# One recurrent layer: the final addition goes into an accumulating transfer, the root becomes logarithm and exponential, small products take rows of their own, and a turn stands amid the gate

## What is computed

```python
xa = _ln(x, ln1_w, ln1_b)
sx = shifted(xa) - xa
t = tanh((xa + sx * maa_x) @ maa_w1).reshape(B, L, 5, -1)          # 5 groups of 32
mw, mk, mv, mr, mg = (t[:, :, j] @ maa_w2[j] for j in range(5))     # the mixtures
xw, xk, xv, xr, xg = (xa + sx * (maa_j + mj) ...)
w = exp(-exp(time_decay + tanh(xw @ decay_w1) @ decay_w2))          # 64 wide inside
r, k, v, g = xr @ Wr.T, xk @ Wk.T, xv @ Wv.T, silu(xg @ Wg.T)
# per head of 16: s_new = k v + w * s ; out = r . (faaaa * k v + s)
y = (y - gm) * rsqrt(gv + EPS) * gn_w + gn_b
x = x + y * g @ Wo.T
xc = _ln(x, ln2_w, ln2_b); sxc = shifted(xc) - xc
rr = sigmoid((xc + sxc * fmaa_r) @ fWr.T)
kk = square(relu((xc + sxc * fmaa_k) @ fWk.T))
x = x + rr * (kk @ fWv.T)
```

## Time and profile before

| what | us |
|---|---|
| median of 3 runs | 3539.14 |
| lowest, highest | 3535.2, 3544.54 |
| the profiled execution, its own time | 3535.91 |
| its span | 3534.1 |
| granted TensorE clock, mean | 0.968 |
| busy in the span: PE, DVE, ACT, POOL | 3319.9, 2390.6, 1787.9, 196.2 |
| this layer | about 1400 to 2320 of the span |

### The profile page before, as it was taken

The page is one execution under the profiler, slowest core; times in us unless marked ns, Lnnn a source line. Parts: engine busy times, 40 slices in busy tenths (PEclk is TensorE's granted clock), DMA queues, the critical chain, the costliest instruction groups (busy, mean ns, idle before and its releaser), DMA issues. The chain is left out here.

```text
span 3534.1 us, 55156 instructions
## 1 busy us (share of the span) xinstructions
PE 3319.9 (94%) x21472; PEld 2547.0 (72%) x21472; DVE 2390.6 (68%) x3781; ACT 1787.9 (51%) x4255; POOL 196.2 (6%) x311
## 2 busy tenths in 40 slices
PE   7999999999999997889999998679999999699998
PEld 6777888887777785656666665357788788488885
DVE  6666666666665665499999999637777887642213
ACT  4555444444454443456565554427777777532222
POOL 0000000000000000000000000001111111000000
PEclk9999999999999999899999999879999999899999
DMA  5332212231122211544444444120001110210004
GB/s 215 124 105 107 108 72 76 97 115 72 72 96 90 78 73 57 156 114 103 111 108 102 114 103 108 41 108 3 35 31 70 44 48 31 88 53 24 24 12 162
DMA packets 93456, 296.08 MB, mean 84 GB/s; under 512 B 20016, under 2 KB 28208, under 8 KB 68752
## 3 DMA queue, kind: packets, MB, share of 16 engines
q1 hardware_dynamic: 64896, 186.47, 18.0%
q0 software_dynamic: 10368, 75.50, 5.6%
q10 hardware_dynamic: 17936, 30.59, 2.5%
HBM read 233.82 MB, written 58.72 MB: 83 GB/s over the span
## 5 line engine op out<-in xcount | busy, mean ns | idle before, releaser
L537 ACT ACTIVATE l_prob<-l_bank,l_nmax 128x512 f32<-128x512 f32 x512 | 345.3, 687 | 276.8 <-DVE l_nmax L679 276.8
L679 DVE TENSOR_REDUCE l_nmax<-l_bank 128x1 f32<-128x512 f32 x512 | 317.5, 682 | 71.4 <-PE l_bank L409 71.2
L375 PE MATMUL l_bank<-l_x_hi,l_w_hi 128*128 128x256 f32 x1024 | 298.0, 291 | 11.7 <-DVE l_x_lo L779 11.7
L702 DVE COPY l_probT<-l_bank 128x512 f32<-128x512 f32 x256 | 173.7, 689 | 175.3 <-PE l_bank L423 173.2
L375 PE MATMUL l_bank<-l_x_hi,l_w_lo 128*128 128x256 f32 x1024 | 290.9, 284 | 0.0
L375 PE MATMUL l_bank<-l_x_lo,l_w_hi 128*128 128x256 f32 x1024 | 290.7, 284 | 0.0
L1752 DVE TENSOR_TENSOR_SCAN l_kv<-l_wx,l_kv 128x2056 f32<-128x2056 f32 x64 | 283.8, 4434 | 1.6 <-DVE first_nrs L1765 1.2
L2320 ACT ACTIVATE l2a_sc<-l2a_sc,l2a_nmax 128x256 f32<-128x256 f32 x512 | 254.8, 508 | 41.1 <-DVE l2a_nmax L2436 41.1
L423 PE MATMUL l_bank<-l_ident,l_prob 128*128 128x128 f32 x2048 | 247.9, 275 | 10.7 <-DVE l_k_lo L695 6.3
L423 PEld LDWEIGHTS l_bank<-l_ident,l_prob 128*128 128x128 f32 x2048 | 225.8, 141 | 24.4 <-DVE l_k_lo L695 16.3
L445 PE MATMUL l_bank<-l_probT,l_v 128*64 128x512 f32 x1024 | 233.8, 598 | 0.0
(11 more groups left out here) (353 smaller groups left out, 8207.5 us busy)
## 6 DMA issues: line engine op xcount, KB each, us to landing
l_vb<-vd SPq DMA_DIRECT2D x64, 1024.0 KB
l_w_hi<-kept_w_hi POOLq DMA_DIRECT2D x24, 1024.0 KB, 8.2
l_w_lo<-kept_w_lo POOLq DMA_DIRECT2D x24, 1024.0 KB, 10.2
l_wv_hi<-kept_wv_hi POOLq DMA_DIRECT2D x12, 1024.0 KB, 5.1
l_wv_lo<-kept_wv_lo POOLq DMA_DIRECT2D x12, 1024.0 KB, 7.1
kept_w_hi<-l_w_hi SPq DMA_DIRECT2D x8, 1024.0 KB, 8.8
kept_w_lo<-l_w_lo SPq DMA_DIRECT2D x8, 1024.0 KB, 11.2
l2a_x<-x SPq DMA_DIRECT2D x16, 512.0 KB, 3.8
```

Source lines behind the costliest of these rows:

```text
L375: mm = pe.matmul(s.ap[:, c * ROWS:(c + 1) * ROWS], a[:, kt, c, g, :], b[:, kt, c * ROWS:(c + 1) * ROWS], start=m == 0, stop=m == 3 * KT - 1)
L537: act.activation(prob[h][:, it, :], s.ap[:, :], ACT.Exp, bias=nmax[:, n % 2, it, h:h + 1], accum_out=rsum[:, n % 2, it, h:h + 1]).then_inc ...
L679: dve.tensor_reduce(nmax[:, n % 2, it, h:h + 1], s.ap[:, :], AX.X, ALU.max, negate=True).then_inc(max_ready, 1)
L702: dve.tensor_copy(probT[0][:, j, :], s.ap[:, :]).then_inc(s.drained, 1)
```

## The change

Five edits, all in `l1_layer`:

- **Transfer.** The sum `xres` (x plus the Wo product) is stored to `x2` by ACT as soon as it is made (`store_res`, ahead of `stats_c`), the product rr * (kk @ fWv) is written by `out_part` to `rv`, a view of the tile `sxc`, and POOL issues a transfer that adds `rv` to `x2` in memory (`add_out`, at the end of its round, after waits for `res_stored` and `rv_ready`). DVE's addition L1872 and ACT's `store` go. `shift_c`, which writes `sxc`, now waits for that transfer of the round before.
- **Logarithm.** `roots` takes Ln and then Exp with scale -0.5 on ACT; DVE's reciprocal `inverse` goes.
- **Row halves.** `decay_w1` is held twice side by side, so that `decay_in` gives its 64 results in partitions 0 to 63 and again in 64 to 127, and `decay_out` takes its first half of channels from rows 0 to 63 and the other from rows 64 to 127, in turn.
- **Turning amid the gate.** The turn of xc stands between the two halves of `project g` on PE, and so in `ring`.
- **Mixtures of v and g together.** v lies in rows 64 to 95; g moves from rows 64 to 95 of `w2b` and `tT` to rows 0 to 31, and the products of the two alternate, where mixture v stood.

```diff
-        ring += [f"mv{p}_0", f"mv{p}_1"] if p is not None else []
+        ring += [f"m{n}{p}_{half}" for half in H2 for n in "vg"] if p is not None else []
         ring += [f"bn{r}_0", f"bn{r}_1"] if r is not None else []
-        ring += [f"mg{p}_0", f"mg{p}_1"] if p is not None else []
         ring += [f"nc{q}_0", f"nc{q}_1"] if q is not None else []
         ring += [f"o{c}_0", f"o{c}_1"] if c is not None else []
         ring += [f"v{p}_0", f"v{p}_1"] if p is not None else []
         ring += [f"nv{q}"] if q is not None else []
         ring += [f"mw{p}_0", f"mw{p}_1"] if p is not None else []
+        ring += [f"g{p}_0"] if p is not None else []
         ring += [f"xc{c}_0", f"xc{c}_1"] if c is not None else []
-        ring += [f"g{p}_0", f"g{p}_1", f"mk{p}_0", f"mk{p}_1", f"d{p}"] if p is not None else []
+        ring += [f"g{p}_1", f"mk{p}_0", f"mk{p}_1", f"d{p}"] if p is not None else []
...
-        dw1 = ph.sb("dw1", [P, CT, 64])
+        dw1, dw2 = ph.sb("dw1", [P, CT, P]), ph.sb("dw2", [P, ROWS])
...
+        rv = sxc[:, :, :].rearrange("p c t -> p (c t)").rearrange("p (r n) -> p r n", r=RT)
...
-                        sp.wait_ge(out_stored, 16 * c)
+                        sp.wait_ge(res_stored, 16 * c)
...
+                def add_out(c):
+                    pool.wait_ge(res_stored, 16 * (c + 1))
+                    pool.wait_ge(rv_ready, 2 * c + 2)
+                    pool.dma_start(x2[c].rearrange("(r p) n -> p r n", p=P), rv, accum_op=ALU.add).then_inc(out_added, 16)
...
+                    if b >= 1:
+                        add_out(b - 1)
+                pool.wait_ge(out_added, 16 * B)
...
-                def mixture(p, n):
-                    f = MIX.index(n)
-                    lhs, own, at = (w2a, slice(32 * f, 32 * f + 32), 0) if f < 4 else (w2b, slice(64, 96), 1)
+                def mixture(p, *names):
+
                     pe.wait_ge(t_ready, p + 1)
                     for half in H2:
-                        s = S[f"m{n}{p}_{half}"]
-                        free(pe, s)
+                        for n in names:
+                            free(pe, S[f"m{n}{p}_{half}"])
                         for ct in (2 * half, 2 * half + 1):
-                            mm = pe.matmul(s.ap[:, ct % 2 * ROWS:(ct % 2 + 1) * ROWS], lhs[own, ct * P:(ct + 1) * P], tT[own, at, :],
-                                           start=True, stop=True)
-                        mm.then_inc(s.full, 1)
+                            for n in names:
+                                f, s = MIX.index(n), S[f"m{n}{p}_{half}"]
+                                lhs, own, at = (w2a, slice(32 * f, 32 * f + 32), 0) if f < 4 else (w2b, slice(0, 32), 1)
+                                mm = pe.matmul(s.ap[:, ct % 2 * ROWS:(ct % 2 + 1) * ROWS], lhs[own, ct * P:(ct + 1) * P], tT[own, at, :],
+                                               start=True, stop=True)
+                                if ct % 2:
+                                    mm.then_inc(s.full, 1)
...
-                        mm = pe.matmul(s.ap[0:64, 0:ROWS], dw1[:, kt, :], xf[1][:, kt, :], start=kt == 0, stop=kt == CT - 1)
+                        mm = pe.matmul(s.ap[:, 0:ROWS], dw1[:, kt, :], xf[1][:, kt, :], start=kt == 0, stop=kt == CT - 1)
...
                 def decay_out(p):
                     drained(pe, S[f"d{p}"])
                     for half in H2:
-                        s = S[f"w{p}_{half}"]
-                        free(pe, s)
-                        for ct in (2 * half, 2 * half + 1):
-                            mm = pe.matmul(s.ap[:, ct % 2 * ROWS:(ct % 2 + 1) * ROWS], w2b[0:64, ct * P:(ct + 1) * P], tT[0:64, 1, :],
+                        free(pe, S[f"w{p}_{half}"])
+                    for i in H2:
+                        for half in H2:
+                            s, own = S[f"w{p}_{half}"], slice(64 * half, 64 * half + 64)
+                            mm = pe.matmul(s.ap[:, i * ROWS:(i + 1) * ROWS], dw2[own, i * P:(i + 1) * P], tT[own, 1, :],
                                            start=True, stop=True)
-                        mm.then_inc(s.full, 1)
+                            if i == 1:
+                                mm.then_inc(s.full, 1)
...
-                        mixture(p, "v")
+                        mixture(p, "v", "g")
                     if now:
                         if b == 0:
                             pe.wait_ge(mats_in, 96)
                         picks(PER * b + 1)
                         bonus(b)
-                    if 0 <= p < B:
-                        mixture(p, "g")
...
+                    if 0 <= p < B:
+                        project(p, "g", (0,))
                     if c >= 0:
                         pe.wait_ge(cxn_ready, c + 1)
                         turn(f"xc{c}", tmp_rows)
                     if 0 <= p < B:
-                        project(p, "g")
+                        project(p, "g", (1,))
                         mixture(p, "k")
                         decay_in(p)
...
-                        act.wait_ge(out_ready, c)
...
-                    act.activation(rs[:, :], s.ap[:, 0:ROWS], ACT.Sqrt, bias=eps[:, 0:1]).then_inc(s.drained, 1)
+                    act.activation(rs[:, :], s.ap[:, 0:ROWS], ACT.Ln, bias=eps[:, 0:1]).then_inc(s.drained, 1)
+                    drained(act, s)
+                    act.activation(rs[:, :], rs[:, :], ACT.Exp, scale=-0.5).then_inc(rs_ready, 1)
...
-                def store(c):
-                    act.wait_ge(out_ready, c + 1)
-                    act.dma_start(x2[c].rearrange("(r p) n -> p r n", p=P), xres[:, :, :]).then_inc(out_stored, 16)
+                def store_res(c):
+                    for half in H2:
+                        drained(act, S[f"o{c}_{half}"])
+                    act.dma_start(x2[c].rearrange("(r p) n -> p r n", p=P), xres[:, :, :]).then_inc(res_stored, 16)
...
-                    if c >= 1:
-                        store(c - 1)
...
                     if c >= 0:
+                        store_res(c)
                         stats_c(c)
...
-                def inverse(c):
-                    drained(dve, S[f"var{c}"])
-                    dve.reciprocal(rs[:, :], rs[:, :]).then_inc(rs_ready, 1)
...
+                        dve.wait_ge(out_added, 16 * c)
...
-                        dve.tensor_tensor(tmp_rows[:, half, :], s.ap[:, :], tmp_rows[:, half, :], ALU.mult).then_inc(rv_ready, 1)
+                        dve.tensor_tensor(rv[:, half, :], s.ap[:, :], tmp_rows[:, half, :], ALU.mult).then_inc(rv_ready, 1)
...
-                    dve.tensor_tensor(xres[:, :, :], xres[:, :, :], tmp_rows, ALU.add).then_inc(out_ready, 1)
...
-                        if n == 1 and c >= 0:
-                            inverse(c)
...
-    d["l1_w1"], d["l1_dw1"] = by_rows(w["maa_w1"]), by_rows(w["decay_w1"])
-    d["l1_w2"], d["l1_dw2"] = w["maa_w2"].reshape(160, COLS), w["decay_w2"]
+    d["l1_w1"], d["l1_dw1"] = by_rows(w["maa_w1"]), by_rows(np.concatenate([w["decay_w1"], w["decay_w1"]], axis=1))
+    d["l1_w2"] = w["maa_w2"].reshape(160, COLS)
+    d["l1_dw2"] = np.concatenate([w["decay_w2"][:, :ROWS], w["decay_w2"][:, ROWS:]], axis=0)
```

More of the change, by code:

```diff
@@ L912, with l1_layer @@
 MIX = ["w", "k", "v", "r", "g"]
-def l1_layer(nc, first, d, att, x1, u, vd, x2):
+def l1_layer(nc, kept, first, d, att, x1, u, vd, x2):
     HS, NJ, PER, CG = 16, 8, 8, 32
@@ L996, in l1_layer @@
         s0_in, vb_in = [ph.sem(f"s0_in{i}") for i in range(2)], [ph.sem(f"vb_in{i}") for i in range(NV)]
-        v_stored, out_stored = ph.sem("v_stored"), ph.sem("out_stored")
+        v_stored, res_stored = ph.sem("v_stored"), ph.sem("res_stored")
+        out_added = kept.enter_context(nc.semaphore("kept_out_added"))
         summed, dev_in, dev_ready = ph.sem("summed"), ph.sem("dev_in"), ph.sem("dev_ready")
@@ L1083, in _ @@
                 sp.dma_start(w2a[:, :], d["l1_w2"][0:P, :]).then_inc(w2_in, 16)
-                sp.dma_start(w2b[64:96, :], d["l1_w2"][P:160, :]).then_inc(w2_in, 16)
-                sp.dma_start(w2b[0:64, :], d["l1_dw2"]).then_inc(w2_in, 16)
+                sp.dma_start(w2b[0:32, :], d["l1_w2"][P:160, :]).then_inc(w2_in, 16)
+                sp.dma_start(dw2[:, :], d["l1_dw2"]).then_inc(w2_in, 16)
                 for n in ("Wv", "Wg"):
@@ L1200, in first @@
                     for kt in range(CT):
[L1201 removed]
+                        mm = pe.matmul(s.ap[0:32, ROWS:2 * ROWS], w1[:, kt, P:160], xf[0][:, kt, :], start=kt == 0, stop=kt == CT - 1)
                     mm.then_inc(s.full, 1)
[L1204 to L1206 removed]
+                def mixture(p, *names):
                     pe.wait_ge(t_ready, p + 1)
                     for half in H2:
[L1209 to L1210 removed]
+                        for n in names:
+                            free(pe, S[f"m{n}{p}_{half}"])
                         for ct in (2 * half, 2 * half + 1):
[L1212 to L1214 removed]
+                            for n in names:
[5 more added lines that the diff above has]
```

(9 more changed lines are left out.)

3 lines of the change are left out of this document (1 added, 2 removed).

## The result

| | before | after |
|---|---|---|
| median of 5 runs each, on one chip | 3540.64 | 3558.33 |
| lowest, highest | 3535.2, 3544.54 | 3557.13, 3559.35 |
| span of the profiled execution | 3534.1 | 3555.3 |
| granted TensorE clock, mean | 0.968 | 0.959 |

The ratio is 1.0060, 95% interval 1.0049 to 1.0072: slower by 17.7 us in the medians and by 21.2 between the two spans. Round 3 went from 102.37 to 106.13. DVE lost 2.5 us of work in it and PE 0.2, and both wait longer: DVE 9.1 us instead of 2.8, PE 6.0 instead of 2.0. Windows of the kernel after: length; busy of PE, PEld, DVE, ACT, POOL; granted clock, DMA share, GB/s. The second line is `decay_in`, the third `fWk`.

The account below looks back on a forecast made before the run. The round, 102.37 us, was taken to close over four legs through PE, DVE and ACT. At +2.65 per full round, 10.6 + 4.1 - 1 - 2 + 1 = +12.7 gave 3551 against 3539.14; forecast range 3541 to 3560, overall 3524 to 3564.

Parts of the forecast that it names:

- leg D: PE alone, `decay_in` to the next `picks`, 38.81 us: `decay_out` -1.0, low clock after PE's idle +2.4 per full round.
- Leg A: `picks` on PE to `first_input` on DVE, 11.85 us: ACT's second load and second function add 1.8.
- The rival of the drain: On ACT ahead of `first_input`: each change of function also drains ACT, 1.4 more in six rounds, 3559; chance 0.04.
- Leg C: `shift_c` on DVE to `decay_in` on PE, 5.50 us: `decay_in` waits for Silu of the gate's first half, +1.15.
- rival 1: PE's clock stays up, or falls only while PE stands: six times 2.4 less, 3537, no change; chance 0.24.
- Leg B: DVE alone, `first_input` to `shift_c`, 46.21 us: the reciprocal leaves, -1.7, to 44.5.
- rival 3: At `decay_out`: groups of rows don't run side by side, so its gain falls away, 3559; chance 0.06.
- The idle at `decay_in`: PE waiting for Silu ahead of `decay_in`: 3.0, plus about 1.7 as the old wait's low clock goes, 4.7 us.
- Rounds 6 and 7 and the end: Last rounds: reciprocals -3.3, later `fWv` +2.3, together -1; layer's end with POOL's transfer +1, bounds -1 to +4.
- Round 1: First full round, about 100.3 us out of an emptier pipeline, so some 1.4 more to lose: +4.1.
- Rival 2: At `first_input` and `scale_rows`: DVE sets the pace, so the removed reciprocal and addition count, 3519; chance 0.18.
- Rival 4: Added transfer delays loads of `vb`, or `shift_c` waits for it: 2 us in each of 7 rounds, 3565; chance 0.06.

Follow-up runs that it names:

- e3: Changed kernel with the banks in `ring` dealt out as before, turn amid the gate kept in PE's order: 3526.2 us, ratio 0.9958.
- e1: Changed kernel with the turn of xc ahead of the whole gate again, in PE's order and in `ring`: 3537.4 us, ratio 0.9993.
- e9: Kernel before with only the turn amid the gate added, banks in the changed kernel's order: 3559.7 us, ratio 1.0067.
- e4: Changed kernel with Exp and its table load moved behind `first_part` on ACT: 3545.9 us, ratio 1.0021.
- e11: Changed kernel with the gate's second half made twice on PE in the full rounds, same result: 3543.2 us, ratio 1.0020.
- e10: Changed kernel with banks as before, Exp behind `first_part`, and the variances' one-column products ahead of the projection of v: 3513.3 us, ratio 0.9934.
- e8: Changed kernel without the transfer, DVE adding to xres and ACT storing it as before: 3559.5 us, ratio 1.0057.

## Why the prediction was right, and where its sum was not

The forecast was the slightly slower case, 3551 in 3541 to 3560; it is 3558.3. The direction and the main mechanism, the bank and Silu, were right; the size was 7 us short, and it would have been shorter still if two errors had not made up for each other in leg D (an idle taken too long, and a price per idle that its own rows did not bear). Step by step:

- **Leg A**, +1.8: +1.73 measured. The rival of the drain would have been +3.2. The Ln starts 1.29 after its load, the second load 0.02 after Ln has ended: the trace has the load's 1.28 that the Trainium skill gives ("ScalarE: Activation LUTs", What ACT_TABLE_LOAD costs), and no room for its drain of about 1380 ns. The sum by the rows was right.
- **Leg C**, `decay_in` 6.65 after `shift_c`: 6.65 in round 3, 6.66 on average, released by Silu. The mechanism is confirmed by e3.
- **Leg D**, clock +2.4 and `decay_out` -1.0: `decay_out` gave 0.80 (e1's leg D against before's) and the clock cost 1.98 (39.99 against 38.01); in e9 the clock's term was 2.63. The size is near, but partly by luck. I had taken 2.4 from an idle of 5.28 and put it on `picks` and `fWk`. The idle in after is 2.97 to 3.85, and by my own rows the nearest case, 3.75, had cost nothing. And the loss falls elsewhere: `decay_in`, which stands first behind the idle, takes 3.38 to 3.78 instead of 1.99, `picks` behind it 1.07 to 1.76 in rounds 2 to 5 and `fWk` its usual 7.07. So my sign "`picks` near 1.9, with 1.07 rival 1 holds" looked at the wrong product: in round 4 `picks` takes 1.07, and `decay_in` is slow all the same. Rival 1 (the clock stays up) and rival 3 (row groups don't run side by side, 1.14 against 1.99) are out.
- **Leg B**, -1.7: this is the step that failed: -0.33 instead of -1.7. I took the reciprocal off and stopped there, though I had leg A longer by 1.8: PE then stands ahead of `first` for 2.12 instead of 0.39, the low clock makes `first` and its second part 1.6 longer, `spread_rs` comes late, and DVE waits 1.15 and 0.17 at `scale_y` where the reciprocal had stood. It is what I had reckoned with in leg D (PE stands, then runs slow), not applied at the second place where PE stands. It does not happen each time: in round 5 `first` ran at 1.97 behind the same idle, and leg B was 43.87, shorter than forecast. In round 4 `shift_c` waits 1.35 more for a late turn. In e4 and e11, where `first` runs at 1.97, leg B is 44.29 and 43.86. The row of round 5:

```profile
1999.49 1.97 PE L1209 MATMUL l_bank<-l_xf,l_w 128*128 128x256 f32 x8 [2.12 <-DVE l_xf L1804]
```

- **The idle at `decay_in`**, 4.7: 3.85 in round 3, 2.97 to 3.85 over the rounds. The step "since the low clock goes too that followed the old wait" was wrong. The wait at the turn went, and `picks` and the gate's first half are slow without it: the low clock there comes behind the one-column products and mixture w, and is not seen when they are moved apart (e10). In e9, in the rounds where that stretch ran at the full clock, the idle was 4.77 to 5.28, as long as I had said.
- **Rounds 6 and 7 and the end**, -1 and +1: +1.8 and +3.1. Of the 2.8 that are missing ahead of the end, 1.6 is leg B of round 6 once more: -0.1 there instead of -1.7. The transfer's end was sized by half of a load's landing (4.1); the last transfer lands 5.7 after its issue, which itself comes 1.2 after the last half of `out_part` starts. It costs 2.8, within my bounds of -1 to +4.
- **Round 1**, +4.1: +4.0. **The start**, -2: -2.8.
- **Rival 2** (DVE sets the pace) did not happen. e10 is a kernel in which it does, by three further edits (banks, Exp, variances); the estimate was 3519, and e10 took 3513.
- **Rival 4** is out by e8: without the transfer the rounds are no shorter (105.85 against 105.74).
- **The chances** of no change and of slower add up to 0.40 and 0.42, not to the 0.38 and 0.44 that I wrote.

The sum was 12.7, the spans say 20.8 at the layer's end. Of the 8 that are missing, 4.1 are in rounds 2 to 5, by leg B, 2.8 in rounds 6 and 7 and 2.1 at the end, less 0.9 at the start and in round 1.
